# A two-layer gated cross-attention kernel: layer 0's score matmuls move to 64-row tiles, and its start is reordered

## The reference, cut to what matters

```python
xn = layernorm(x)                                  # per query
q, k, v = xn @ Wq + bq, ctx @ Wk + bk, ctx @ Wv + bv   # 16 heads of width 8
w = softmax(q_h @ k_h.T / sqrt(8) [+ mask in layer 1])
x = x + tanh(g_xattn) * (concat_h(w @ v_h) @ Wo + bo)
h = layernorm(x); gates = top-2 of softmax/sigmoid(h @ gate)
x = x + tanh(g_ffn) * sum_e gates_e * (gelu(h @ W1_e + b1_e) @ W2_e + b2_e)
```

## Time and profile before

| | |
|---|---|
| median of 3 runs | 1044.85 us (1041.06 to 1046.26) |
| the profiled execution: its own time | 1040.23 us |
| its span, first to last instruction | 1038.1 us |
| busy PE / DVE / ACT / POOL | 922.5 / 723.0 / 586.2 / 525.0 us |
| granted TensorE clock, mean | 0.981 of full speed |

### The profile page before, as it was taken

One profiled execution on the slowest core, in us unless ns is written; L12 is line 12 of the kernel. 1 busy time (PEld: TensorE's weight loads), 2 busy tenths in 40 slices (PEclk: granted clock), 3 DMA queues, 4 the chain that ended last, 5 costly groups with the idle time before them and its releaser, 6 DMA issues.

```text
span 1038.1 us, 32346 instructions
## 1 busy us (share of the span) xinstructions
PE 922.5 (89%) x13088; PEld 675.9 (65%) x13088; DVE 723.0 (70%) x1531; ACT 586.2 (56%) x1060; POOL 525.0 (51%) x667
## 2 busy tenths in 40 slices
PE   2487899999999999999999999999999999999974
PEld 0154577777777777777777777666666666666753
DVE  3376576785767768586785867878787878787722
ACT  1044556556565565656547565665757575757560
POOL 5353445543546335453446565665657576672202
PEclk9998899999999999999999999999999999999995
DMA  8735653333323333233465646767676767665200
GB/s 181 133 90 137 145 126 72 72 83 69 63 55 85 70 77 76 37 81 70 95 137 88 143 110 132 162 123 156 124 152 122 145 130 146 137 137 97 52 2 18
DMA packets 95215, 107.24 MB, mean 103 GB/s; under 512 B 22394, under 2 KB 86972, under 8 KB 95068
## 3 DMA queue, kind: packets, MB, share of 16 engines
q1 hardware_dynamic: 95068, 105.19, 49.0%
HBM read 35.89 MB, written 0.46 MB: 35 GB/s over the span
## 4 chain that ended last, share of the span: by engine, by line
PE 66%; DVE 16%; ACT 9%; issue 5%; SPq 2%; DMA 1%; POOL 0%; POOLq 0%; ACTq 0%; DVEq 0%
PE pO L993 13%; PE pMX L1010 12%; PE pST L972 12%; PE pKV L1124 6%; PE pFY L1082 6%; PE pKV L1115 5%; PE pFH L1150 5%; DVE mx L925 4%; DVE mx L920 4%; ACT P L678 3%; DVE rden L839 3%; PE pFY L1047 2%; ACT HR L715 1%; PE pFY L1086 1%; ACT V L696 1%
## 5 line engine op out<-in xcount | busy, mean ns | idle before, releaser
L678 ACT ACTIVATE P<-pST 125x448 f32<-125x448 f32 x768 | 396.1, 542 | 349.9 <-PE pST L972 344.3
L925 DVE TENSOR_REDUCE mx<-pMX 112x1 f32<-112x500 f32 x384 | 258.4, 673 | 172.3 <-PE pMX L1010 172.1
L1010 PE MATMUL pMX<-kop,qmax 104*112 104x500 f16 x768 | 293.1, 392 | 44.7 <-DMA qmax<-qlo 18.5
L972 PE MATMUL pST<-qexp,kop 106*128 106x112 f16 (+1 forms) x3072 | 280.2, 214 | 19.9 <-ACT P L678 9.3
L972 PEld LDWEIGHTS pST<-qexp,kop 106*128 106x128 f16 (+1 forms) x3072 | 209.9, 102 | 127.1 <-issue 42.9
L920 DVE TENSOR_REDUCE mx<-pMX 112x1 f32<-112x500 f32 x384 | 255.8, 666 | 42.8 <-PE pMX L1010 41.9
L993 PE MATMUL pO<-P,V 125*17 125x112 f32 x6144 | 186.0, 262 | 0.0
L993 PEld LDWEIGHTS pO<-P,V 125*17 125x17 f32 x6144 | 136.8, 98 | 46.2 <-issue 36.3
L1010 PEld LDWEIGHTS pMX<-kop,qmax 104*112 104x112 f16 x768 | 99.0, 132 | 93.1 <-issue 21.7
L563 POOL CAST khi<-kfull 128x500 f16<-128x500 f32 x96 | 57.7, 601 | 193.0 <-ACT kfull L691 192.8
L565 POOL TENSOR_TENSOR klo<-kfull,khi 128x500 f16<-128x500 f32 x96 | 109.0, 1135 | 7.8
(11 more groups left out here) (144 smaller groups left out, 1089.6 us busy)
## 6 DMA issues: line engine op xcount, KB each, us to landing
C<-in_ctxT SPq DMA_DIRECT2D x32, 750.0 KB, 6.2
kop<-khi SPq DMA_DIRECT2D x192, 125.0 KB
kop<-maskop SPq DMA_DIRECT2D x48, 437.5 KB
kop<-klo SPq DMA_DIRECT2D x96, 125.0 KB
qexp<-qmax SPq DMA_DIRECT2D x32, 182.0 KB
maskin<-in_mask SPq DMA_DIRECT2D x8, 656.2 KB, 6.2
kop<-maskop SPq DMA_DIRECT2D x2, 1312.5 KB
qmax<-qhi SPq DMA_DIRECT2D x128, 7.0 KB
```

Source lines behind the costliest of these rows:

```text
L678: nc.scalar.activation(P[0:KP, slot, h * 4 * T:(h + 1) * 4 * T], pST[0:KP, h, 0:4 * T], ACT.Exp, scale=EXP_SCALE).then_inc(exp_done, 1)
L925: nc.vector.tensor_reduce(mx[:, s % 2, m // PAIRS, m % PAIRS:m % PAIRS + 1], pMX[0:T, 1, 0:CW], AX.X, ALU.max).then_inc(max_done, 1)
L972: mm = nc.tensor.matmul(pST[0:cols, h, i * T:(i + 1) * T], kop[0:ROWS, b, p, tile * KP:tile * KP + cols], qexp[0:ROWS, b, p, :, :].rearran ...
L1010: nc.tensor.matmul(pMX[0:T, m % 2, 0:CW], qmax[0:SHIFT0, st.s % 2, p, :, :].rearrange("r j q -> r (j q)"), kop[0:SHIFT0, st.s % 2, p, c * ...
```

## The change

Layer 0 loses its mask rows: a head pair has 48 rows for a maximum and 50 for a score. Head pairs 0 to 3 lie in rows 0 to 49 and head pairs 4 to 7 in rows 64 to 113 of the same buffers, so each of these matmuls has a tile of 64 rows, in the lower or the upper half of the array. In a layer 0 step (`together`) PE issues a maximum of one half next to the score half of the other, twice, then the weighted sums, then the projection. In layer 1 the order stays, but for kt 10 of even steps. The other parts:

- DVE writes the queries block-diagonal in both layers (four operations for two), so `qmax` takes six transfers in layer 0 and three in layer 1; `kop` takes six for each third in layer 0 (three before), `qexp` two, the maxima's rows two.
- Layer 0's gelu is in four parts, at kt 9 instead of 8; `y0` waits for one part and `y1` for two. Experts are paired in order of the parts. In steps with a feed-forward part the value projections stand at kt 7, 8, 10, and the last is evicted ahead of the exponentials.
- The first loads stand in order of need: key weights, the first 112 rows of `x`, the first context in three pieces, then the rest. ACT's queue takes biases, the first queries, the two subtraction rows (`shift_rows`) and the attention output weights.

```diff
-        uses += [(8, "v0", 1), (9, "v1", 1), (10, "v2", 1)]
+        first = 7 if has_f(s) else 8
+        uses += [(first, "v0", 1), (first + 1, "v1", 1), (10, "v2", 1)]
...
-        uses += [(4, "qT", 2), (5 if s < 0 else 6, "q", 1)]
+        uses += [(2, "qT", 2), (3, "q", 2)] if s < 0 else [(4, "qT", 2), (6, "q", 2)]
...
+def experts_of(l, i):
+
+    if l == 0:
+        return 2 * i, 2 * i + 1
     e = 4 * (i // 2) + i % 2
     return e, e + 2
+
...
+        def queries(eng, n):
+
+            for row, part in ((0, qhi), (PR, qhi), (2 * PR, qlo)):
+                if layer_of(n) == 0:
+                    for h in range(2):
+                        at = HALF * h + row
+                        eng.dma_start(qmax[at:at + PR, n % 2, 0:HP, :, :],
+                                      part[HALF * h:HALF * (h + 1), n % 2, :, :]).then_inc(qmax_in, 16)
+                else:
+                    eng.dma_start(qmax[row:row + PR, n % 2, :, :, :], part[:, n % 2, :, :]).then_inc(qmax_in, 16)
+            if opens_layer(n):
+                eng.dma_start(qmax[MASK0:SHIFT0, n % 2, :, :, :].rearrange("s p j q -> s (p j) q"),
+                              pick[:, :].unsqueeze(1).broadcast_to([S, H, S])).then_inc(qmax_in, 16)
...
-            sp.dma_start(W[:, :], wpack).then_inc(w_in, 16)
-            sp.dma_start(bq_row[:, :], bqrow).then_inc(w_in, 16)
-            sp.dma_start(bc[:, :], bcast.partition_broadcast(128)).then_inc(w_in, 16)
-            sp.dma_start(C[:, :], ctxT[0]).then_inc(c_in, 16)
-            sp.dma_start(X[:, :].rearrange("t (g d) -> t g d", g=G),
-                         x.rearrange("(g t) d -> t g d", g=G)).then_inc(x_in, 16)
-            sp.wait_ge(init_v, 1)
-            sp.wait_ge(init_p, 5)
-            for b in range(2):
-                sp.dma_start(kop[MASK0:SHIFT0, b, :, :],
-                             maskop[0:S, :].unsqueeze(1).broadcast_to([S, PAIRS, S2])).then_inc(init_dma, 16)
-                for i in range(2):
-                    sp.dma_start(kop[SHIFT0 + i:SHIFT0 + i + 1, b, :, :],
-                                 shift_rows[:, i:i + 1, :].broadcast_to([1, PAIRS, S2])).then_inc(init_dma, 16)
-                sp.dma_start(qmax[MASK0:SHIFT0, b, :, :, :],
-                             pick[:, :, :].rearrange("s (p j) q -> s p j q", j=2)).then_inc(init_dma, 16)
+            sp.dma_start(W[:, 0:D], wpack[:, 0:D]).then_inc(wk_in, 16)
+            sp.dma_start(xg(0), x[0:T, :]).then_inc(x0_in, 16)
+            for c in range(CH):
+                sp.dma_start(C[:, c * CW:(c + 1) * CW], ctxT[0, :, c * CW:(c + 1) * CW]).then_inc(c0_in[c], 16)
+            sp.dma_start(W[:, D:], wpack[:, D:]).then_inc(w_in, 16)
+            sp.dma_start(X[:, D:].rearrange("t (g d) -> t g d", g=G - 1),
+                         x[T:, :].rearrange("(g t) d -> t g d", g=G - 1)).then_inc(x_in, 16)
+            sp.dma_start(bc[:, :], bcast.partition_broadcast(128)).then_inc(bc_in, 16)
...
                 for row, part in ((0, khi), (PR, klo), (2 * PR, khi)):
-                    sp.dma_start(kop[row:row + PR, dst, :, cols], part[:, cols]).then_inc(kop_in[c], 16)
+                    if n < B:
+                        for h in range(2):
+                            at = HALF * h + row
+                            sp.dma_start(kop[at:at + PR, dst, 0:HP, cols], part[HALF * h:HALF * (h + 1), cols]
+                                         ).then_inc(kop_in[c], 16)
+                    else:
+                        sp.dma_start(kop[row:row + PR, dst, :, cols], part[:, cols]).then_inc(kop_in[c], 16)
...
+                    if layer_of(s) == 0:
+                        for h in range(2):
+                            rows = slice(HALF * h, HALF * h + SHIFT0_L0)
+                            sp.dma_start(qexp[rows, s % 2, 0:HP, :, :], qmax[rows, s % 2, 0:HP, :, :]
+                                         ).then_inc(qexp_in[s % 2], 16)
+                    else:
+                        sp.dma_start(qexp[0:SHIFT0, s % 2, :, :, :], qmax[0:SHIFT0, s % 2, :, :, :]
...
+            def early_loads(s, kt):
+
+                if s == -1 and kt == 5:
+                    act.wait_ge(fh_free, upto(fh_uses, s, "q", True))
+                    queries(act, 0)
+                if s == 0 and kt == 0:
+                    act.wait_ge(init_p, 2)
+                    for b in range(2):
+                        for h in range(2):
+                            row = HALF * h + SHIFT0_L0
+                            act.dma_start(kop[row:row + 2, b, 0:HP, :].rearrange("r p (i n) -> r (p i) n", n=SHW),
+                                          shift_rows[:, :].unsqueeze(1).broadcast_to([2, HP * S2 // SHW, SHW])
+                                          ).then_inc(init_dma, 16)
+                if s == 0 and kt == 11:
...
+                for kt in range(KT):
+                    side_by_side = has_m(s) and layer_of(s) == 0
+                    if has_f(s) and kt == 10:
+                        evacuate(kt)
+                    early_loads(s, kt)
+                    exps(st, kt, 0)
+                    if not side_by_side and not (has_f(s) and kt == 10):
+                        evacuate(kt)
                     exps(st, kt, 1)
+                    if side_by_side and not (has_f(s) and kt == 10):
+                        evacuate(kt)
...
-                    if kt == 8 and has_f(s):
+                    if kt == 9 and has_f(s):
                         act.wait_ge(fh_free, st.at(lambda s: before(fh_uses, s + 1, True)))
                         if layer_of(s - 3) == 0:
-                            for half in (HR[:, 0:E0 * F0C // 2, :], HR[:, E0 * F0C // 2:, :]):
-                                nc.scalar.activation(half, half, ACT.Gelu).then_inc(gelu_done, 1)
+                            for part in range(4):
+                                two = HR[:, 2 * F0C * part:2 * F0C * (part + 1), :]
+                                nc.scalar.activation(two, two, ACT.Gelu).then_inc(gelu_done, 1)
...
+            def low_context(c):
+
                 cols = slice(c * CW, (c + 1) * CW)
                 dve.wait_ge(init_chi, c + 1)
-                nc.vector.tensor_tensor(Clo[:, 0, cols], C[:, cols], Chi[:, 0, cols], ALU.subtract).then_inc(init_c, 1)
...
+            def query_weights():
+
+                dve.wait_ge(bias_in, 16 * 5)
+                nc.vector.tensor_scalar(bkp[:, :], bkp[:, :], QK_SCALE, None, ALU.mult).then_inc(init_b, 1)
+                nc.vector.tensor_scalar(bq_row[:, :], bq_row[:, :], QK_SCALE, None, ALU.mult).then_inc(init_b, 1)
+                dve.wait_ge(w_in, 16)
+                scaled("wq0", 2 * D).then_inc(init_v, 1)
+                dve.wait_ge(init_v, 3)
+                dve.wait_ge(init_k, 2)
+                nc.vector.tensor_copy(w("wk0").rearrange("d (h r p) -> d h r p", r=PR, h=2),
+                                      w("wq0").rearrange("d (r h p) -> d h r p", r=PR, h=2)).then_inc(init_b, 1)
+
...
+                        q = pFH[:, 0:T].rearrange("p (b q) -> p b q", b=2)
+                        own = head_of[:, layer_of(s + 1), :]
+                        for j in range(2):
+                            link(nc.vector.tensor_scalar(qhi[:, :, j, :], q, own[:, j:j + 1], None, ALU.mult))
+                        for j in range(2):
+                            nc.vector.scalar_tensor_tensor(out=qlo[:, :, j, :], in0=q, scalar=own[:, j:j + 1],
+                                                           in1=qhi[:, :, j, :], op0=ALU.mult, op1=ALU.subtract
+                                                           ).then_inc(fh_free, 1)
...
+                    if s == -1 and kt == 1:
+                        low_context(0)
+                        query_weights()
+                        low_context(1)
+                    if s == -1 and kt == 2:
+                        low_context(2)
+                    if s == -1 and kt == 5:
+                        other_weights()
...
+                if h == 0:
+                    score_operands(n, tile)
+                b, keys = n % 2, keys_of(tile)
+                if n > 0 or tile > 0:
+                    pe.wait_ge(exp_done, 2 * (KT * n + tile) + h - 1)
+                for i in range(HP):
+                    if layer_of(n) == 0:
+                        rows, slot = slice(HALF * h, HALF * h + ROWS_L0), i
+                    else:
+                        rows, slot = slice(0, ROWS), HP * h + i
+                    mm = nc.tensor.matmul(pST[0:keys.stop - keys.start, h, i * T:(i + 1) * T],
+                                          kop[rows, b, slot, keys],
+                                          qexp[rows, b, slot, :, :].rearrange("r j q -> r (j q)"),
                                           start=True, stop=True)
                 mm.then_inc(st_ready, 1)
...
+                if layer_of(n) == 0:
+                    h = 1 - m % 2
+                    rows, slot = slice(HALF * h, HALF * h + SHIFT0_L0), i // 2
+                else:
```

(44 more changed lines are left out.)

328 lines of the change are left out of this document (192 added, 136 removed).

## The result

The changed kernel took 1032.1 us (median of 14 runs, 1029.7 to 1040.6), the kernel before 1045.1 beside it (14 runs, 1041.0 to 1049.6): ratio 0.9885, 95% interval 0.9861 to 0.9909. The forecast was 975, the range 955 to 1008. The profiled execution of the changed kernel took 1031.1 us; the prediction's sum was 974, so 57 us are to be explained. A ratio leaves out the runs of a kernel that are over 1.5% above its fastest, which matters in experiments 2 and 6.

A forecast was written before the change was run, and what follows sets the result against it. PE's issue was taken to bound layer 0. From 1040.2 us: start -20, layer 0 -46.5, step 16 +3.6, gelu -1, layer 1 -2 gave 974, about 975 against the median; eight-in-ten range 955 to 1008.

The forecast's parts named there:

- PE's own work: Layer 0 steps: PE's work alone would be 25.9 us in an odd step and 28.0 in an even one.
- a change of tile shape: PE, layer 0: each switch costs 0.105 us; 17.6 us more in steps 1 to 15, 3.6 in step 16.
- DVE's gate: Layer 0: PE only two maxima ahead of DVE; odd steps 27.3 us, even 29.4, with DVE setting kt 5 to 8.
- kt 0 to 4 and 9 to 11 stay PE's: Odd layer 0 step: PE, not DVE, sets these places, 18.2 us where they took 21.5.
- these stay: Steps 1 to 3: big weight transfers ahead of `qexp<-ct`, causing step 2's 4.0 us stall, remain; gain 6.5 us.
- signs of being wrong that were named: Late scores, PE idle before maxima over 3 us a step, clock below full in steps 4 to 15, late `kop`.
- The start: Start and step 0: 20 us less, ends 12 and 24; first maximum near 21 us, step 0 shorter by 2 or 3.
- Gelu and values: Even layer 0 steps: `y0`'s 1.2 us wait for the gelu goes; gain at most 1 us a step.
- Step 16: First step with layer 1's maxima: 3.6 us more, from 53 switches of tile shape instead of 19.
- Steps 17 to 31: Steps 17 to 19 1 us less; steps 20 to 31 2 us less, bounds 3 more and 6 less.
- the no-overlap rival: Layer 0 maxima and score halves on PE don't overlap at all: 1032 us, faster by 0.8%; chance 0.07.
- The rival at 1012: Layer 0: short matmuls can't pass the long one, only 0.12 us less a place: 1012 us; chance 0.08.

The follow-up runs named there:

- experiment 2: Changed kernel with each layer 0 maximum in the same array half as the score half issued behind it: 1051.0 us, ratio 1.0096 to the kernel before.
- experiment 6: Changed kernel with large weight loads issued behind `qexp<-ct` and key projections of steps 0 to 14 at kt 1, 3, 5: 1012.3 us, ratio 0.9687.
- experiment 3: Changed kernel with the second maximum and score half of a layer 0 place moved behind the weighted sums and projection: 1064.3 us, ratio 1.0210.
- experiment 1: DVE reduces 250 of each maximum's 500 columns: changed kernel 993.8 us, ratio 0.9545; kernel before 1016.1 us, ratio 0.9747.
- experiment 4: Changed kernel with key projections of steps 0 to 14 at kt 1, 3, 5 instead of 2, 4, 6: 1026.3 us, ratio 0.9821.
- Experiment 5: Large weight loads of steps 1 to 3 issued behind the next step's `qexp<-ct`: changed kernel 1019.7 us, ratio 0.9753; kernel before 1031.9, 0.9890.
- experiment 8: On top of experiment 6, step 0's projection between the maxima, step 16's two score halves last, side by side: 1011.5 us, ratio 0.9712.

## Why the prediction was wrong

**PE's own work: right.** An even step was put at 28.0 us of PE and an odd one at 25.9. Measured: 28.0 busy in step 6 (28.8 once maxima are short), and 25.9 in step 7 once maxima are short. Full overlap, 0.41 us a place, is what the timeline shows; what the sum calls a change of tile shape came out at 0.10 us in step 7 of the changed kernel (0.15 from the last product of the values to a pair, where these products start 0.055 apart) and at 0.09 behind a projection in experiment 3 (0.30 where 0.21 is usual). No record names a tile shape: that these gaps belong to a change of it, and the counts of changes behind the 17.6 and 3.6 us, are the author's reading of the operands, and no run shows them; the runs show the gaps and PE's busy time of a step.

**DVE's gate: the step that failed.** The prediction found the right resource and the right limit ("PE can be only two of them ahead"), and then applied it to one stretch, kt 5 to 8 of an odd step, and as a lump of idle time elsewhere: 27.3 and 29.4 us. Measured 29.97 and 31.63, which is 24 us over the ten steps 6 to 15. In an odd step the stretch that was watched came out as forecast, 9.0 us for 9.1; it is the sentence "kt 0 to 4 and 9 to 11 stay PE's" that failed, 21.0 us for 18.2. With two banks the limit holds place by place: a place lasts as long as the slower of PE and DVE needs for it, and the change moved both maxima of a place to its front, where DVE's slack falls behind them. For odd steps, 13 of the 24 us, experiments 1 and 4 show this: with short maxima the odd step falls by 2.6 us, about what the forecast missed. For even steps, the other 11 us, they do not. There the term that was too small is DVE's idle time (6.0 us in the sum, 8.7 of 31.6 in step 6), but short maxima leave the step at 31.9, so the cause is more than the maxima and stays open.

**Steps 1 to 5: 21 us over, and "these stay" is part of it.** The stalls did not all stay: the one of step 3 grew from 3.5 to 4.8 us and that of step 4 from 0.8 to 2.9, since PE now comes to kt 3 earlier while `qexp<-ct` still lands behind the weights; only the one of step 2 stayed (4.05 and 4.07 us). With each come 6.8 to 10.2 us at the lower clock level; the two before had 6.8 each, and the sum counted no change in this. Experiment 5 takes 17.9 us out of steps 2 to 4 here and 9.4 in the kernel before, so the stalls and their clock cost 8.5 us more than they did. The rest of the 21 is the gate, the slow pace in step 1 and 3.4 us at the lower level in step 5, which no run tells apart. The clock below full in steps 4 and 5 (6.8 and 3.4 us) is one of the signs of being wrong that were named; PE idle before maxima for over 3 us a step is not seen. Step 1, 3.7 us longer, has some 10 us of the start's slow pace in it, 3.4 us more at the lower level, and 4.6 us of waits for maxima where it had 2.5. The forecast had nothing for that pace.

**The start: size off by 5.7 us.** The first maximum is at 22.08 us for a forecast of 21 (38.11 before):

```profile
12.69 0.77 PE L1342 MATMUL pFH<-xnqT,W 128*128 128x112 f32 x2 [4.00 <-DVE keepT L948]
22.08 0.67 PE L1183 MATMUL pMX<-kop,qmax 48*112 48x500 f16 x2 [4.37 <-DMA qmax<-qlo]
```

But step 0 was to get 2 or 3 us shorter and got 1.8 longer: its maxima run together ahead of the projection, and then the projection runs while DVE has nothing queued, 2.54 us at kt 2 where it was 2.26, and PE's waits for maxima in step 0 rose from 2.2 to 4.3 us. That looks like the gate again, but experiment 8, which put the projection between the maxima, did not shorten it. The 2 us of latency in the sum were an assumption. In the changed kernel the 64 KB of the key weights landed 2.0 us after their issue, and the first maximum started 2.2 us after the last issue of queries had ended (19.84 us); in the kernel before, transfers of 0.2 to 56 KB landed in 1.6 to 2.8 us.

**Gelu and values:** 0.73 us an even step for a forecast of at most 1: right. **Step 16:** +2.1 for +3.6: right in sign, a little small. **Steps 17 to 31:** 2.0 more for 3 less; inside the bounds of both terms. **SP's queue:** no maximum of steps 6 to 15 waits for a DMA of `kop`: right. **Rivals:** the time of the no-overlap rival (1032) is what was measured, and for the wrong reason: the timeline shows full overlap. That the two agree is luck: 70 us of overlap are there, and 57 us of misses elsewhere hide most of them. The rival at 1012, in which the long matmul holds the short ones back, is not what the starts show: the last of four short matmuls starts 0.16 us after the long one, whose record is 0.41 us long. The ends in the trace are modelled, so they say nothing for or against it. On DVE's side nothing came with the overlap: a reduction takes 0.67 us in both kernels.

**Left open:** what bounds even steps once the maxima are short (31.9 us, PE busy for 28.8), and why the clock falls for 3.4 us at the same place of some later steps and not of others.
